# DLRM tower on one core: the step of four tiles split into two halves

## What is computed

```python
sd = jnp.einsum('bfd,bd->bf', sparse_values, dense_features)
ss = jnp.einsum('bfd,bgd->bfg', sparse_values, sparse_values)
pairs = ss[:, iu, ju]                                  # iu, ju: triu_indices(26, k=1)
z = jnp.concatenate([dense_features, sd, pairs], axis=1)
h = jnp.concatenate([z, r_dense_features], axis=1)     # 128 + 26 + 325 + 128 columns
h = jnp.maximum(h @ W_top1 + b_top1, 0.0)              # 512
h = jnp.maximum(h @ W_top2 + b_top2, 0.0)              # 256
y = h @ W_top3                                         # 1
```

## Time and profile before

| | |
|---|---|
| device time, three runs | 557.14, 558.03, 558.73 us; the median is 558.03 us |
| the profiled execution | 554.1 us |
| its span | 552.2 us |
| mean granted TensorE clock in it | 0.805 |
| PE busy | 375.6 us, 68% of the span |
| POOL busy | 277.3 us, 50% |
| DVE busy | 231.4 us, 42% |
| ACT busy | 174.7 us, 32% |

### The profile page before, as it was taken

How to read it: one execution, slowest core, us unless ns; L and a number is a source line. 1 busy time by engine, 2 the same in 40 slices (tenths; PEclk the granted TensorE clock), 3 DMA queues, 4 the chain that set the end, 5 groups by cost and what they waited for, 6 DMA issues and landing times.

```text
span 552.2 us, 12229 instructions
## 1 busy us (share of the span) xinstructions
PE 375.6 (68%) x5424; PEld 294.6 (53%) x5424; DVE 231.4 (42%) x579; ACT 174.7 (32%) x221; POOL 277.3 (50%) x297
## 2 busy tenths in 40 slices
PE   2650587426379959955489859954559859975697
PEld 0430455315267648745367647743448648864576
DVE  5610687414144553532244443632226535505500
ACT  1400345313132343421142333421215324443122
POOL 7777467563416656753516756663416666610000
PEclk9985599667579979976579969965569978996699
DMA  8522263110102112211101112211101111100000
GB/s 201 142 53 52 67 198 89 40 49 23 40 8 53 44 38 53 66 35 37 40 10 52 44 38 52 63 43 30 27 20 40 43 43 49 43 18 4 4 0 1
DMA packets 11596, 26.93 MB, mean 49 GB/s; under 512 B 5033, under 2 KB 5161, under 8 KB 11409
## 3 DMA queue, kind: packets, MB, share of 16 engines
q0 software_dynamic: 9216, 18.89, 13.4%
q1 hardware_dynamic: 2328, 7.27, 4.9%
HBM read 26.14 MB, written 0.01 MB: 47 GB/s over the span
## 4 chain that ended last, share of the span: by engine, by line
PE 62%; issue 21%; ACT 7%; another core or an unknown queue 7%; DMA 2%; POOL 1%; DVE 1%
PE sum_bank L410 22%; PE vec_bank L436 12%; PE work_bank L462 8%; PE vec_bank L426 6%; PE work_bank L472 5%; ACT vecT L316 3%; PE work_bank L458 3%; PE work_bank L481 2%; ACT vecT L310 2%; PE work_bank L450 2%; PE id_bank L396 1%; DMA rows<-in_tbl,ids_all 1%; ACT parts L296 1%; ACT late L342 1%
## 5 line engine op out<-in xcount | busy, mean ns | idle before, releaser
L221 POOL DMA_INDIRECT rows<-in_tbl,ids_all x288 | 274.6, 953 | 207.7 <-PE vec_bank L426 86.5
L253 DVE TENSOR_TENSOR onehot<-id_bank,row_f 125x1024 fp32r<-125x1024 f32 x128 | 151.6, 1220 | 170.6 <-PE sum_bank L410 72.8
L410 PE MATMUL sum_bank<-onehot,parts 125*128 125x512 f32 x512 | 166.0, 459 | 4.2 <-DVE onehot L253 4.2
L436 PE MATMUL vec_bank<-vecT 128*26 128x26 f32 x4096 | 68.7, 215 | 81.4 <-issue 73.7
L410 PEld LDWEIGHTS sum_bank<-onehot,parts 125*128 125x128 f32 x512 | 103.1, 213 | 30.8 <-issue 12.2
L316 ACT COPY vecT<-vec_bank 128x512 f32<-128x512 f32 x72 | 85.3, 1200 | 80.7 <-remote 49.0
L436 PEld LDWEIGHTS vec_bank<-vecT 128*26 128x26 f32 x4096 | 56.4, 131 | 96.4 <-issue 85.0
L264 DVE STREAM_TRANSPOSE late<-late 128x832 f32<-128x832 f32 x16 | 28.7, 1793 | 113.6 <-ACT late L325 113.6
L426 PE MATMUL vec_bank<-ident,rows 128*128 128x128 f32 x288 | 52.1, 314 | 10.6 <-DMA rows<-in_tbl,ids_all 3.8
L325 ACT COPY late<-vec_bank 128x416 f32<-128x416 f32 x32 | 16.2, 507 | 123.1 <-PE vec_bank L436 123.1
L426 PEld LDWEIGHTS vec_bank<-ident,rows 128*128 128x128 f32 x288 | 41.2, 162 | 23.9 <-issue 11.7
(11 more groups left out here) (23 smaller groups left out, 99.2 us busy)
## 6 DMA issues: line engine op xcount, KB each, us to landing
rows<-in_tbl,ids_all POOLq DMA_INDIRECT x288
late<-in_tbl SPq DMA_DIRECT2D x8, 480.0 KB
w_all<-in_weights SPq DMA_DIRECT2D x1, 1540.0 KB
xT<-in_dense_t SPq DMA_DIRECT2D x4, 256.0 KB
late<-in_weights SPq DMA_DIRECT2D x1, 256.0 KB
ids_all<-in_ids SPq DMA_DIRECT2D x1, 208.0 KB, 3.0
late<-in_tbl SPq DMA_DIRECT2D x8, 20.0 KB
vecT<-in_ids_t SPq DMA_DIRECT2D x1, 64.0 KB
```

The costliest lines, as they stand in the source:

```text
L221: nc.gpsimd.indirect_dma_start(rows[:, g % ROWS_RING, n, t, :], None, tables[f], bass.IndirectOffsetOnAxis(ids_all[:, TD * d + t, f:f + 1], 0)
L253: nc.vector.tensor_tensor(onehot[:, use % RING, :, :], bass.AP(got.tensor, got.offset, [got.ap[0], [0, PW], [1, QS]]), bass.AP(numbers.ten ...
L410: last = nc.tensor.matmul(sum_bank[into % 2][:], parts[:, part, CH_AT[n] + c0 + c, :], onehot[:, use % RING, c, :], start=(p % PER == 0 an ...
L436: last = nc.tensor.matmul(vec_bank[into % 2][BL * j:BL * j + GC, i * GC:(i + 1) * GC], vecT[:, s, 0:GC], vecT[:, s, 1:VECS], start=True, s ...
```

## The change

The four tiles of a quad are no longer multiplied in one go. After the lookup come the grams of tiles 0 and 1; then a stretch called *between*; then the grams of tiles 2 and 3. The stretch between has twelve steps. It holds the row groups that are left, layer2 and layer3 of the duo *behind* (the second duo of the quad before), and from step 5 the whole MLP of the quad's *own* first duo. The lookup keeps 13 row groups (nine in the first quad), and of the network the pair transposes and layer1 of the duo behind. At the program's end stands the MLP of one duo, and no longer of two.

Two smaller edits go with it. layer3 is written the other way round: the weights are the stationary operand and 256 samples stream, two matmuls for four, and the result is one line of 256 numbers. The lines lie in rows 32 and 64 of a tensor whose rows 0 to 7 hold the ids, and are stored by two transfers for one. DVE turns tiles 0 and 1 ahead of the first six packs of the next quad, and tiles 2 and 3 behind them.

```diff
-    ROWS_IN_A = 15
-    ROWS_AFTER_GRAM = {0: [15], 1: [16, 17]}
-    TURN_AFTER = {RING - 1: [0, 1, 2], RING + 1: [3]}
-    PAIRS_AFTER_GRAM = {2: 0, 3: 1}
+    ROWS_BY_GRAM = [GROUPS] + [13] * (QUADS - 1)
+    BETWEEN = 12
+    LAYER2_BETWEEN = {0: 0, 2: 1}
+    LAYER3_BETWEEN = 4
+    OWN_BETWEEN = 5
+    PAIRS_AFTER = {10: 2, 11: 3}
+    LAYER1_AFTER = {13: 0, 17: 1, 21: 2, 25: 3}
+    def rows_after(q, p):
+        n = ROWS_BY_GRAM[q]
+        return [j for j in range(n) if (2 * j + 1) * (PACKS - 1) // (2 * n) == p]
...
-            sp.dma_start(y.rearrange("(p t) o -> p (t o)", t=TILES), y_cols[:]).then_inc(y_stored, 16)
+            for h in range(2):
+                sp.dma_start(y.rearrange("(p h t) o -> h p (t o)", p=P, h=2)[h:h + 1],
+                             y_half[h].rearrange("o (p t) -> o p t", p=P)).then_inc(y_stored, 16)
...
-                for t in range(TD):
-                    for b in range(M2):
-                        last = nc.tensor.matmul(work_bank[use % 2][:, t:t + 1], h2[:, b, t * P:(t + 1) * P],
-                                                w3_sb[:, b:b + 1], start=(b == 0), stop=(b == M2 - 1))
+                for b in range(M2):
+                    last = nc.tensor.matmul(work_bank[use % 2][0:1, 0:DS], w3_sb[:, b:b + 1], h2[:, b, :],
+                                            start=(b == 0), stop=(b == M2 - 1))
...
-                for t in range(TQ):
-                    if t == TD:
-                        pe.wait_ge(vec_drained, rows_at(q, 2 * GROUPS - 1) + 1)
+                for t in range(TD):
                     for h in range(2):
                         gram(q, t, h)
-                    for j in ROWS_AFTER_GRAM.get(t, []):
+                for step in range(BETWEEN):
+                    for j in ROWS_BETWEEN[q].get(step, []):
                         transpose_rows(q, j)
-                    if t in PAIRS_AFTER_GRAM:
-                        transpose_pairs(q, PAIRS_AFTER_GRAM[t])
-            for p in range(PACKS):
-                mlp(QUADS - 1, p)
+                    if q and step in LAYER2_BETWEEN:
+                        layer2(behind, LAYER2_BETWEEN[step])
+                    if q and step == LAYER3_BETWEEN:
+                        layer3(behind)
+                    if step == OWN_BETWEEN:
+                        for t in range(TD):
+                            transpose_pairs(q, t)
+                        if q == 0:
+                            pe.wait_ge(w1x_summed, 1)
+                    if step >= OWN_BETWEEN:
+                        own_layers(own, step - OWN_BETWEEN)
+                pe.wait_ge(vec_drained, rows_at(q, 2 * GROUPS - 1) + 1)
+                for t in range(TD, TQ):
+                    for h in range(2):
+                        gram(q, t, h)
+            for t in range(TD, TQ):
+                transpose_pairs(QUADS - 1, t)
+            for step in range(M1 + M2 + 1):
+                own_layers(DUOS - 1, step)
```

125 lines of the change are left out of this document (68 added, 57 removed).

## The result

The changed kernel takes **585.81 us** (median of 4 runs, 581.14 to 589.0), the kernel before 558.38 (4 runs, 557.14 to 560.29): a ratio of **1.048**, 95% interval 1.040 to 1.056. It is slower by 4.8%. The prediction was 552 us with a range of 530 to 570, and faster as the likeliest sign: it was slower, and outside the range. The profiled execution has a span of 579.3 us (581.14 us in all) beside 552.2, and what follows explains these 27.1 us.

A forecast was written before the change was run, and what follows sets the result against it. It took PE to set the end, with grams bound by instructions arriving and held up by POOL's gathers. Quads of 175, 119.5, 119.5 and 132 us sum to 546.0, 6.2 under 552.2; as median 552 us, range 530 to 570.

The forecast's parts named there:

- First lookup and first pair: First quad: lookup ends at 102.4 for 111.0 us, then the first pair of grams takes 15 us, to 117.4.
- the full ring of the forecast: First lookup: POOL can issue nine row groups and must stop at about 50.3; an earlier end of the hold-up saves 5 us.
- Between, first quad: Stretch between the first quad's pairs of grams: 26 us, nearer the lower bound of 24 undisturbed.
- my second rival: Betweens of the first three quads: seven late wake-ups of 8.9 us in each 3, 21 us slower, median 573; chance 0.25.
- The undisturbed price (22 to 24 us): Stretch between without late wake-ups: 24 us as lower bound, and 22 to 24 in the last quad, after the gathers.
- my own bounds: Stretch between: lower bound 24 us undisturbed, upper adds one late wake-up of 8.9 us; 26 taken for the first three quads.
- Second pair, first quad: First quad's second pair runs under POOL's gathers with bursts in its pauses, from 143.4 to 175 us.
- Lookup and first pair, later quads: POOL's 13 groups end at 75 us, the pair 1.5 + 2.5 + 2.3 later, at 82; last quad 77.
- POOL does not hold the lookups: Rival: PE reaches the grams with the gathers done; 515 us, or 521 as a median; chance 0.17.
- Second pairs, later quads: Clean pairs beginning with a stored burst of 200 or more records, 11.5 us each.
- no stored burst: Rival: each second pair costs 14.7 us for 11.5, four times: 13 us, median 565; chance 0.08.
- End: After the last gram: turn 4.6, MLP 14.6 and the transfers, 21.5 us for 31.6, since one duo's MLP has gone.

The follow-up runs named there:

- e4: Kernel before, with POOL not issuing row group 8 until pack 12 of the first quad is done: 552.5 us, ratio 1.000.
- e1: Kernel before with only its first six row groups gathered, 66 of 72 left out: 423.4 us.
- e2: Changed kernel with only its first six row groups gathered, 66 of 72 left out: 441.6 us.
- e3: Changed kernel with split grams and moved row groups kept, but the whole MLP back in the next quad's lookup: 577.8 us, ratio 1.044 against the kernel before.
- e17: The kernel of e3 with only its first six row groups gathered: 438.2 us.
- e5: Kernel before, with POOL filling a scratch tile (0.94 us) and waiting for it after each group of four gathers: 555.2 us, ratio 0.993.

## Why the prediction was wrong

Two steps of the sum failed on the slow side. The stretch between was taken at 26, 26, 26 and 22 us, with 2 for a disturbance, and took 45.4, 30.9, 30.3 and 22.1: 28.7 more. And the lookup with the first pair was to end 6.3 us after POOL's run in the later quads, and took 27.4 more in the three of them. The first quad's lookup and pairs came 29.2 us shorter than forecast and hid as much of it. The forecast of the span was 546.0, the measured 579.3: 33.3 us, by terms (from the table):

- **First lookup and first pair: 16.2 less.** I had it end at 117.4, it was 101.2. POOL did stop, from 45.69 to 50.45, and DVE, 13.86 us late for 19.1 in the earlier trace rows, went on at 48.73. But it stopped after eight groups and not after nine, when the buffer for the ninth had been free since group 2 was transposed at 26.14, so the full ring of the forecast is not what stopped it; the trace calls the wait "remote". The hold-up that ends with it was right, its cause was not:

```profile
26.14 0.60 PE L448 MATMUL vec_bank<-ident,rows 128*128 128x128 f32 x4
...
48.73 4.85 DVE L258 TENSOR_TENSOR onehot<-id_bank,row_f 125x1024 fp32r<-125x1024 f32 x4 [13.86 <-remote]
...
50.45 0.94 POOL L226 DMA_INDIRECT rows<-in_tbl,ids_all  x1 [4.75 <-remote]
```

And e4 shows no gain from such a stop alone (ratio 1.000). Without gathers the stage loses 4.3 us (77.1 to 72.8, e1 and e2). I put the rest down to gathers that came later, when the buffers they need were freed later (60 of them were issued by the start of the first pair or just behind it, 76 in the kernel before); no run shows it by itself. That the stage came out so short is luck for the forecast, not a step of it.
- **Between, first quad: 19.4 more.** I took 26 us with 2 for a disturbance. The three late wake-ups shown above sum to 21.15. This is the mechanism of my second rival, at a price of 8.9 us each for one; it was 5.2 to 10.0 for three. In the second and third quad it was 4.9 and 4.3 more, in the last 0.1 more. **The undisturbed price (22 to 24 us) was right, and I chose the wrong end of my own bounds**; in the first quad the upper one, 33, was too low as well: I had argued that PE had other work in its queue at most drains. It had, but not enough for a wake-up that late: PE stood for 5.70, 2.91 and 10.81 us.
- **Second pair, first quad: 13.0 less.** I had it under POOL's run, bursts in its pauses, until 175. It began later (146.6), with POOL at its last group: 18.6 us. The slow stretch between had covered the run; e3, where it doesn't, has this pair at 43.8 us, from 120.1 to 163.9.
- **Lookup and first pair, later quads: 9.2, 10.4 and 7.8 more.** POOL's run ended 77.8 us after the lookup's start in the second quad, where I had 75. (For the last quad my own terms, 69.5 and 6.3, give 76 and not the 77 that I took.) But after it the pair needed 13.4 us, and I had 6.3 since I counted one burst in a pause of POOL before. POOL paused at 233.29, before the pair, which then began with 43 records. This step rested on where a pause happens to fall. The rival "POOL does not hold the lookups" fails too: POOL was still gathering when each first pair began.
- **Second pairs, later quads: 4.6 more in all.** The last began with a burst of 188 records, where I had said 200 or more; the second quad's with 28, 3, and after 2 us 198; the third's with 27 and 3, and after 2 us 242. Still, the rival "no stored burst" put 14.7 us on each, and they took 14.3, 12.2 and 12.6. The last pair, where nothing else runs, is the row to set beside the earlier trace rows; 3 packets came on q8 in it:

```profile
543.40 1.82 PE L458 MATMUL vec_bank<-vecT 128*26 128x26 f32 x188
547.63 1.28 PE L458 MATMUL vec_bank<-vecT 128*26 128x26 f32 x128 [2.41 <-issue]
551.36 1.71 PE L458 MATMUL vec_bank<-vecT 128*26 128x26 f32 x128 [2.45 <-issue]
```

PE stands for 2.4 us ahead of each 128 records. The Trainium skill ("Runtime: NRT & Kernel Launch", "Instruction fetch mechanics") has the cost of crossing from one block of 256 instructions to the next mostly hidden; the trace doesn't agree.
- **End: 1.8 more**, 23.3 for 21.5; PE waits 3.61 us for the turn, and two transfers.

Behind these terms lies a step that I left out: I never summed the order without the gathers. The runs without them show that it has a price by itself, 19.4 us. My own undisturbed terms give, as an estimate, +9: 49.5 us out of the lookups (3.6 + 3 x 15.3) and 10.1 off the end, against stretches of 94 and pairs of 92 (eight of 11.5) where four gram stages of 29.4 stood. That the forecast still came out at -6.2 was the hold-ups that I let the rebuilt quads escape. The rest of the 19.4 is mostly in the pairs: 99.0 us in e2 for my 92. What PE does inside a gram stage is cheap because PE waits there for instructions (3.8 us in e1 beside e17, for 8.0 outside); I had read that from the earlier trace rows and didn't draw it for the three row groups and the two transposes of pairs that the change takes out of the stage. And I charged the lower clock once, 2 us ahead of the MLP, and not to the lookup behind the second pair (2.4 us in e17). Of the 27.1 us, then, 19.4 come without gathers and some 8 with them, which is a difference of runs on two chips and not sharper than a few us.

## What to carry to other kernels

A stage whose engine waits for its instructions is a place to put work, not one to split: here work that cost 3.8 us inside it cost 8.0 outside (with two row groups more), and the lookup behind the split stage ran at a clock of 0.95 for 0.99. Sum the new order without disturbances before asking what it does to them, and ask of each moved piece what it used to hide in. And where one engine's back-to-back operations hold up others, the cost sits wherever the run is; here moving or holding the run moved it and made it larger, and a pause of about 1 us inside the run took away one of its two parts and lengthened the other.

## What was not expected of the hardware

- Kernels that differ only in their gathers: 423.4 us with 6 groups, 550.6 with all 72, though POOL's queue takes only 13.4% of the DMA engines' time in the profile of before, and all queues together move 49 GB/s.
- The same kernel takes 429 to 438 us on two chips and 550 to 563 on the others, with the same time for each gather. The four kernels with all gathers profiled on the first kind have no wait put down to a late wake-up at all.
- POOL's own stop of 2.6 us comes after twelve gathers, but not after each twelve: the runs of the kernels before and after begin with 40 and 32 without a stop, and the first stretch between has 24. With pauses of 1.2 us in each group it doesn't occur at all: in e5 POOL has no wait of that kind left.
- In a gram under a run of gathers PE may do one record in 1.4 to 2.8 us for 29 us (e3).
